# Second phase of a conv-and-FFN kernel: the programs of ACT, GpSimd and SyncE written out for all 32 images

## The chip, the cores and the metric

One core of one Trainium2 chip runs the kernel. The metric is the device time of one execution in microseconds; the kernel before took 2137.33 us, the median of three runs.

## The reference

x is 32 images of 128 channels by 56 x 56. Two residual steps follow each other:

```python
x = x + conv_ref(ln_c(x), w, b, gamma, beta)   # sign(LN over channels) * sign-weights 3x3, batch norm, relu
t = to_tokens(x)                               # 3136 tokens of 128 per image
t = t + ffn_ref(ln_t(t), wr, br, w1, b1, w2, b2)
```

```python
weights = ln_t(t) @ wr + br                    # ffn_ref: router weight per token
sel = the top 1567 tokens of an image by weight
y = gelu(sel @ w1 + b1) @ w2 + b2              # 128 -> 512 -> 128
processed = 0 except y * weight at sel;  result = processed + ln_t(t)
```

The batch norm needs the mean and variance of the convolution over all images, so nothing behind it can begin before all 32 images are convolved.

## The kernel before

Each engine runs a program of its own; semaphores tie them together. Channels lie on the 128 partitions, an image is cut into NCH = 7 chunks of T = 448 tokens. Phase 1 (up to about 500 us) makes the convolution `y` of every image, stores it as f16 in `y_int` and gathers batch statistics. Phase 2 does the rest, image by image, at about 49 us an image.

In phase 2 an order written out by hand rules everything. An image has POS = 56 positions, eight per chunk; in each, TensorE (`PE`) runs `hidden` (L975 to L977: three matmuls of a 128-column block of w1, in two f16 pieces) or `output` (L986). Tables such as RELU_AT, NORM_AT, COUNT_AT say at which position each side job is due: `due(table, shift, n, b, pos)` returns the jobs of image n + shift that fall on `pos`. So while PE multiplies image n, the others prepare images n + 1 and n + 2 and finish n - 1. The side jobs that matter here:

- SyncE (queue `SPq`) in `phase2(n, b)`: writes the statistics rows (three DMAs, L384), writes the router's row to `w_row` (L390), waits until it has landed, loads it back as `wse` for the search (L395) and as `wk` (L397), then loads the second parts of x and y of image n + 2 (L345, L348).
- DVE: `wrow` from the router (L753), then eight rounds of a search for the threshold: `count_above` (L766), summed across partitions by PE (`sum_counts`, L995), `choose`, `raise_end`, `next_candidate` (L772 to L783). Between them it computes token statistics; `mean_over_std` (L714, 112 x 28 elements) reads `stw` and `rm`, and PE's `rows_of_stats` (L951) transposes its result. DVE also forms `base` (L746) and applies the gate (L823).
- GpSimd (`POOL`): `rm` by a power (L444, 4.8 us), `low_part` (L430), `residual` (L425), `add_base` (L437).
- ACT: gelu into `hs` (L517), `yo` out of PSUM (L527), relu into `zr` (L545, which for chunks 0 and 4 waits for the loads of x and y), the f16 copy `th` (L552), and two DMA issues of gate_all (L539).

How each engine runs through the images: `pairs` writes out the images before the third, makes a hardware loop over pairs of images (13 turns, n = 3 to 28) and writes out the last ones. In the loop n is a register, so waits such as `act.wait_ge(h_done, g * NB + j + 1)` need register arithmetic in front of them, and DMA addresses need register moves. Written out, the values are constants in the instructions. DVE's phase 2 is written out for all images already; PE, ACT, GpSimd and SyncE use `pairs`. GpSimd, ACT and SyncE have the same program for image n in either form. Images are named here by the n that PE is working on: PE begins image 1 at about 587 us, image 2 at 637, image 3 at 687, image 16 at 1326, image 28 at 1910, image 29 at 1958.5.

Of the kernel before, what the change touches and what calls it, by code (L numbers as in the profile page):

```python
# [82 lines left out]
def block_kernel(nc, consts, x_in, cw_in, cb_in, gamma_in, beta_in, wr_in, br_in, w1_in, b1_in,  # L83
# [13 lines left out]
    with ExitStack() as ctx:  # L97
# [168 lines left out]
        def wait_count(eng, semaphore, value):  # L266

            if not (isinstance(value, int) and value <= 0):
                eng.wait_ge(semaphore, value)

        def pairs(eng, body, first, last, lo, hi):

            for n in range(lo, first):
                body(n, n % 2)
            turns = (last - first) // 2
            with eng.Fori(0, turns) as k:
                body(k * 2 + first, first % 2)
                body(k * 2 + (first + 1), (first + 1) % 2)
            for n in range(first + 2 * turns, hi):
                body(n, n % 2)  # L280
# [14 lines left out]
        def has(n, low=0, high=n_img):  # L295

            return not is_int(n) or low <= n < high

        def cut(t, c, size=T):
            return t[:, c * size:(c + 1) * size]  # L300
# [3 lines left out]
        def due(table, shift, n, b, pos):  # L304

            steps = [table] if is_int(table) else table
            found = []
            for at, m, mb in ((pos, n + shift, (b + shift) % 2), (pos + POS, n + shift - 1, (b + shift + 1) % 2)):
                if at in steps and has(m):
                    found.append((m, mb, steps.index(at)))  # L310
            return found
# [11 lines left out]
        P2 = (3, n_img - 3)  # L323
# [5 lines left out]
        def _(sp):  # L329
# [73 lines left out]
                    store(n - 1, 1 - b, 0)  # L403
                    store(n - 1, 1 - b, 1)

            pairs(sp, phase2, *P2, -2, n_img + 1)
            for b in range(2):
                sp.wait_ge(out_saved[b], 32 * (n_img // 2))

# [1 line left out]
        @block.gpsimd  # L411
        def _(pool):

            for b in range(2):
                nc.gpsimd.memset(sg[b], 0.0).then_inc(border_clear, 1)
            nc.gpsimd.memset(wsel_h[:, :], 0.0).then_inc(prep_pool, 1)
            nc.gpsimd.memset(wsel_l[:, :], 0.0).then_inc(prep_pool, 1)
            pool.wait_ge(bound_ready, 1)
            nc.gpsimd.tensor_tensor(roots[:, :], norms[:, :], half, ALU.pow).then_inc(bound_rooted, 1)
            pool.wait_ge(var_bn_ready, 1)  # L420
            nc.gpsimd.tensor_tensor(bn_r, bn_ve, kt[:, K_MHALF:K_MHALF + 1], ALU.pow).then_inc(bn_rooted, 1)  # L421

            def residual(n, b, c):
                pool.wait_ge(relu_ready, n * NCH + c + 1)
                nc.gpsimd.tensor_tensor(cut(xb[b], c), cut(xb[b], c), zr[(b + c) % 2][:, :],  # L425
                                        ALU.add).then_inc(x1_ready, 1)

            def low_part(n, b, c):
                pool.wait_ge(th_ready, n * NCH + c + 1)
                nc.gpsimd.tensor_tensor(cut(tl, c), tr[(b + c) % 2][:, :], cut(th, c),  # L430
                                        ALU.subtract).then_inc(tl_ready, 1)

            def add_base(m, b, c):
                g = m * NCH + c
                pool.wait_ge(gated, g + 1)
                pool.wait_ge(base_ready, g + 1)
                nc.gpsimd.tensor_tensor(cut(yo[b], c), cut(yo[b], c), cut(base[b], c),  # L437
                                        ALU.add).then_inc(out_ready, 1)

            def phase2(n, b):  # L440
                for pos in range(POS):
                    for m, mb, _ in due(VAR_AT + 1, 1, n, b, pos):
                        pool.wait_ge(var_ready, m + 1)
                        nc.gpsimd.tensor_tensor(rm[:, 0, :], stw[:, 5, :], kt[0:TILE, K_MHALF:K_END],  # L444
                                                ALU.pow).then_inc(rstd_ready, 1)
                    for m, mb, c in due(RELU_AT, 2, n, b, pos):
                        residual(m, mb, c)
                    for m, mb, c in due(LOW_PART_AT, 1, n, b, pos):
                        if has(m - 1):
                            pool.wait_ge(h_done, ((m - 1) * NCH + c + 1) * NB)  # L450
                            pool.wait_ge(w_done, m)
                        low_part(m, mb, c)
                    for m, mb, c in due([p + 1 for p in OUT_AT], -1, n, b, pos):
                        add_base(m, mb, c)

            pairs(pool, phase2, *P2, -2, n_img + 1)


        @block.scalar
        def _(act):  # L460
# [45 lines left out]
            def phase2(n, b):  # L506
                for pos in range(POS):
                    slot, j = divmod(pos, 2 * NB)

                    if j < NB and has(n):  # L510
                        g = n * NCH + slot
                        act.wait_ge(h_done, g * NB + j + 1)
                        if j == 0:

                            wait_count(act, y_done, g - 1)

                        nc.scalar.activation(hs[(b + slot) % 2][:, j, :], ps[:, H_BANK + j, 0:T],  # L517
                                             ACT.Gelu_apprx_tanh, bias=b1c[:, j:j + 1],
                                             scale=undo[:, 1:2]).then_inc(h_ready, 1)
                    if j == 2 * NB - 1 and (has(n) and slot > 0 or slot == 0 and has(n - 1)):  # L520

                        c = (slot - 1) % NCH
                        m, mb = (n, b) if slot > 0 else (n - 1, 1 - b)
                        act.wait_ge(y_done, m * NCH + c + 1)
                        if c == 0 and has(m - 2):
                            act.wait_ge(out_saved[mb], (m - mb) * 16)
                        nc.scalar.activation(cut(yo[mb], c), ps[:, Y_BANK, 0:T], ACT.Identity,  # L527
                                             bias=b2_c).then_inc(y_taken, 1)
                    for m, mb, _ in due(ROWS_AT, 1, n, b, pos):
                        act.wait_ge(rms_ready, m + 1)  # L530
                        for s in range(PIECES):
                            act.dma_start(rows[32 + s:33 + s, :].rearrange("a (j p) -> a j p", p=TILE),
                                          rms[:, s, 1, :]).then_inc(norm_rows_in, 16)
                    for m, mb, _ in due(GATE_OUT_AT, -1, n, b, pos):
                        act.wait_ge(gate_saved, (m + 1) * 16)
                        if has(m - 1):
                            act.wait_ge(gated, m * NCH)
                        for part in range(2):
                            act.dma_start(gate_all[:, PART[part]], g_dram[bass.ds(m, 1), PART[part]]  # L539
                                          .to_broadcast([C, (HALF, NCH - HALF)[part] * T])).then_inc(gate_in[part], 16)  # L540
                    for m, mb, c in due(RELU_AT, 2, n, b, pos):
                        if c in (0, HALF):
                            act.wait_ge(xy_in[mb][c // HALF], (m - mb) * 16 + 32)
                        wait_count(act, x1_ready, m * NCH + c - 1)
                        nc.scalar.activation(zr[(mb + c) % 2][:, :], cut(y16[mb], c), ACT.Relu,  # L545
                                             bias=bn_t[:, :], scale=bn_s[:, :]).then_inc(relu_ready, 1)
                    for m, mb, c in due(LOW_PART_AT, 1, n, b, pos):
                        if has(m - 1):
                            act.wait_ge(h_done, ((m - 1) * NCH + c + 1) * NB)
                            act.wait_ge(w_done, m)  # L550
                        act.wait_ge(t_ready, m * NCH + c + 1)
                        nc.scalar.activation(cut(th, c), tr[(mb + c) % 2][:, :], ACT.Copy).then_inc(th_ready, 1)  # L552

            pairs(act, phase2, *P2, -2, n_img + 1)

# [504 lines left out]
```

## Time and profile before

| | us |
|---|---|
| three runs, median (lowest, highest) | 2137.33 (2133.52, 2137.93) |
| the profiled execution's own time | 2127.27 |
| its span | 2125.5 |
| PE busy | 1994.1 (94%) |
| DVE / ACT / POOL busy | 1666.4 / 1211.1 / 933.1 |

The profiled execution is 10 us shorter than the median of the runs, 1.8 us of its time lie outside the span. A busy PE in the table is modelled: ends of matmuls overlap the starts of the next, so differences between starts are the safer measure.

### The profile page before, as it was taken

How to read it: one execution, taken by the hardware profiler on the slowest of the kernel's cores; microseconds unless marked ns; L12 is line 12 of the kernel's file. 1: busy time of each engine (PE TensorE's matmuls, PEld its weight loads, DVE VectorE, ACT ScalarE, POOL GpSimd, SP SyncE). 2: the span in 40 equal slices, each digit the busy share in tenths (PEclk: the TensorE clock that was granted, in tenths of full speed). 3: DMA queues.
4: the chain of work that ended last, by engine and by line, in shares of the span. 5: the costliest groups of instructions: out<-in, count | busy, mean ns of one | idle time of the engine just before them, and what ended most of it. 6: DMA issues, size and time to landing. Idle time of an engine off the chain costs nothing. (4 is left out here: it accounts for less than half of the span.)

```text
span 2125.5 us, 35828 instructions
## 1 busy us (share of the span) xinstructions
PE 1994.1 (94%) x9515; PEld 1021.8 (48%) x9515; DVE 1666.4 (78%) x4766; ACT 1211.1 (57%) x2030; POOL 933.1 (44%) x714
## 2 busy tenths in 40 slices
PE   7999999995899999999999999999999999999995
PEld 4555555552444444444444444444444444444442
DVE  6777777775688888877788888888877888888875
ACT  4444444443656566666666666666666656666652
POOL 1000000003455556655556565556655656565543
PEclk9999999997899999999999999999999999999998
DMA  4434344443123332333333333333333333333213
GB/s 163 178 140 181 142 176 154 163 162 111 51 102 122 131 119 111 126 127 112 112 128 117 124 115 124 114 134 111 127 125 112 125 120 129 111 124 124 99 69 124
DMA packets 68726, 267.91 MB, mean 126 GB/s; under 512 B 22352, under 2 KB 27184, under 8 KB 64688
## 3 DMA queue, kind: packets, MB, share of 16 engines
q1 hardware_dynamic: 55264, 214.90, 27.5%
q10 hardware_dynamic: 13392, 52.29, 6.6%
q14 instruction: 52, 0.43, 0.1%
q8 instruction: 18, 0.29, 0.1%
HBM read 188.08 MB, written 77.87 MB: 125 GB/s over the span
## 5 line engine op out<-in xcount | busy, mean ns | idle before, releaser
L986 PE MATMUL ps<-hs,w_c 128*128 128x448 f32 x1792 | 763.7, 553 | 0.6 <-ACT yo L527 0.6
L517 ACT ACTIVATE hs<-ps,b1c,undo 128x448 f32<-128x448 f32 x896 | 609.2, 718 | 127.2 <-PE ps L977 123.4
L986 PEld LDWEIGHTS ps<-hs,w_c 128*128 128x128 f32 x1792 | 313.4, 190 | 208.6 <-issue 176.9
L889 PE MATMUL ps<-yo,cwT 128*128 128x448 bf16 x2016 | 408.7, 355 | 0.0
L430 POOL TENSOR_TENSOR tl<-tr,th 128x448 f16<-128x448 f32 x224 | 244.0, 1090 | 310.5 <-PE ps L977 192.9
L425 POOL TENSOR_TENSOR xb<-xb,zr 128x448 f32<-128x448 f32 x224 | 261.3, 1168 | 269.2 <-ACT zr L545 267.8
L975 PE MATMUL ps<-th,w_h 128*128 128x448 f16 x896 | 319.2, 356 | 19.8 <-ACT hs L517 19.7
L976 PE MATMUL ps<-tl,w_h 128*128 128x448 f16 x896 | 317.1, 354 | 0.0
L977 PE MATMUL ps<-th,w_l 128*128 128x448 f16 x896 | 317.0, 354 | 0.0
L437 POOL TENSOR_TENSOR yo<-yo,base 128x448 f32<-128x448 f32 x224 | 277.7, 1247 | 77.8 <-DVE yo L823 77.8
L527 ACT ACTIVATE yo<-ps,cols 128x448 f32<-128x448 f32 x224 | 141.5, 632 | 241.7 <-PE ps L986 241.4
L889 PEld LDWEIGHTS ps<-yo,cwT 128*128 128x128 bf16 x2016 | 185.9, 97 | 193.5 <-issue 24.3
L494 ACT ACTIVATE y<-ps 128x448 f16<-128x448 f32 x224 | 121.6, 543 | 258.9 <-PE ps L889 258.9
L545 ACT ACTIVATE zr<-y,bn_t,bn_s 128x448 f32<-128x448 f16 x224 | 169.2, 756 | 144.0 <-DMA y<-y_int 128.6
L605 DVE BATCH_NORM_STATS2 base<-y 128x448 f16 (+1 forms) x224 | 140.2, 627 | 118.5 <-ACT y L494 109.0
L729 DVE TENSOR_TENSOR ur<-xb,ps 128x448 f32<-128x448 f32 x224 | 138.5, 618 | 107.5 <-PE ps L966 100.6
L691 DVE BATCH_NORM_STATS2 st<-ps 112x6 f32<-112x128 f32 x896 | 195.1, 282 | 14.3 <-PE ps L931 10.3
L823 DVE TENSOR_TENSOR yo<-yo,gate_all 128x448 f32<-128x448 f32 x224 | 198.0, 887 | 7.9 <-DMA gate_all<-gate_row 7.9
L421 POOL TENSOR_TENSOR sm<-sm,kt 128x1 f32<-128x1 f32 x1 | 0.6, 564 | 452.3 <-DVE sm L679 452.3
L552 ACT ACTIVATE th<-tr 128x448 f16<-128x448 f32 x224 | 129.0, 576 | 106.3 <-DVE tr L738 91.9
L746 DVE SCALAR_TENSOR_TENSOR base<-tr,xb 128x448 f32<-128x448 f32 x224 | 186.7, 834 | 1.2
L444 POOL TENSOR_TENSOR rm<-stw,kt 112x28 f32<-112x28 f32 x32 | 153.5, 4797 | 34.4 <-DVE stw L709 34.4
(132 smaller groups left out, 2324.2 us busy)
## 6 DMA issues: line engine op xcount, KB each, us to landing
xb<-x SPq DMA_DIRECT2D x31, 1568.0 KB, 7.6
xb<-x SPq DMA_DIRECT2D x33, 896.0 KB, 4.5
gate_all<-gate_row ACTq DMA_DIRECT2D x32, 896.0 KB, 4.3
result<-yo SPq DMA_DIRECT2D x32, 896.0 KB, 3.5
y_int<-y SPq DMA_DIRECT2D x32, 784.0 KB, 3.6
xb<-x SPq DMA_DIRECT2D x33, 672.0 KB, 4.3
gate_all<-gate_row ACTq DMA_DIRECT2D x32, 672.0 KB, 5.5
result<-yo SPq DMA_DIRECT2D x32, 672.0 KB, 3.0
```

Of the source, the lines that this page charges most:

```text
L425: nc.gpsimd.tensor_tensor(cut(xb[b], c), cut(xb[b], c), zr[(b + c) % 2][:, :], ALU.add).then_inc(x1_ready, 1)
L430: nc.gpsimd.tensor_tensor(cut(tl, c), tr[(b + c) % 2][:, :], cut(th, c), ALU.subtract).then_inc(tl_ready, 1)
L437: nc.gpsimd.tensor_tensor(cut(yo[b], c), cut(yo[b], c), cut(base[b], c), ALU.add).then_inc(out_ready, 1)
L517: nc.scalar.activation(hs[(b + slot) % 2][:, j, :], ps[:, H_BANK + j, 0:T], ACT.Gelu_apprx_tanh, bias=b1c[:, j:j + 1], scale=undo[:, 1:2]) ...
L691: last = V.bn_stats(st[:, c * TPG + i, :], ps[0:TILE, BC0 + c % 2, i * C:(i + 1) * C])
L746: V.scalar_tensor_tensor(cut(base[b], c), tr[ring][:, :], 1.0 / T_SCALE, cut(xb[b], c), ALU.mult, ALU.add).then_inc(base_ready, 1)
L823: V.tensor_tensor(cut(yo[b], c), cut(yo[b], c), cut(gate_all, c), ALU.mult).then_inc(gated, 1)
L889: last = M(bank, cwT[:, t, :], sg[b][:, c * ROWS + dy:c * ROWS + dy + ROWS, dx:dx + SIDE], start=t == 0, stop=t == TAPS - 1)
L975: M(bank, w1_h[:, blk], cut(th, c), start=True, stop=False)
L976: M(bank, w1_h[:, blk], cut(tl, c), start=False, stop=False)
L977: M(bank, w1_l[:, blk], cut(th, c), start=False, stop=True).then_inc(h_done, 1)
L986: last = M(bank, w2_c[:, j, :], hs[(b + c) % 2][:, j, :], start=first, stop=final)
```

## The change

Three calls of `pairs` in phase 2 become plain Python loops. The engines SyncE, GpSimd and ACT then have no hardware loop there and no register values; all three programs hold the instructions of 35 or so steps one after the other. TensorE's program is as before (13 turns), DVE's too, and phase 1 is not touched.

```diff
@@ SyncE @@
-            pairs(sp, phase2, *P2, -2, n_img + 1)
+            for n in range(-2, n_img + 1):
+                phase2(n, n % 2)
@@ GpSimd @@
-            pairs(pool, phase2, *P2, -2, n_img + 1)
+            for n in range(-2, n_img + 1):
+                phase2(n, n % 2)
@@ ACT @@
-            pairs(act, phase2, *P2, -2, n_img + 1)
+            for n in range(-2, n_img + 1):
+                phase2(n, n % 2)
```

## Rows read from the trace of the kernel before

**Rows 1.** The page: span, and TensorE's busy time with its instructions.

```profile
span 2125.5 us, 35828 instructions
...
PE 1994.1 (94%) x9515; PEld 1021.8 (48%) x9515; DVE 1666.4 (78%) x4766; ACT 1211.1 (57%) x2030; POOL 933.1 (44%) x714
```

**Rows 2.** Waits from 687 to 1958 us: total us, times, longest us.

```profile
PE ps L995 <- DVE junk L766: 35.9, 31, 1.6
...
PE ps L975 <- ACT hs L517: 17.3, 13, 1.9
...
PEld ps L951 <- DVE rm L714: 0.3, 1, 0.3
```

**Rows 3.** The loops' own line, ACT's branch: ns min/median/max, first and last start.

```profile
L276 ACTq COMPARE_BRANCH  x27: 40/45/54, 99.3 to 1960.4; - x27
```

**Rows 4.** Timeline of SyncE's queue, image 2 (written out).

```profile
660.67 2.62 SPq L384 DMA_DIRECT2D rows<-rms  x3
...
665.87 0.69 SPq L395 DMA_DIRECT2D wse<-w_row  x1
...
667.54 0.43 SPq L348 DMA_DIRECT2D y<-y_int  x1
```

**Rows 5.** Timeline of SyncE's queue, image 16 (in the loop).

```profile
1349.28 2.60 SPq L384 DMA_DIRECT2D rows<-rms  x3
...
1354.75 0.73 SPq L395 DMA_DIRECT2D wse<-w_row  x1
...
1356.80 0.35 SPq L348 DMA_DIRECT2D y<-y_int  x1
```

**Rows 6.** Timeline, ACT and PE, image 16: a late landing of y.

```profile
1364.35 0.76 ACT L545 ACTIVATE zr<-y,bn_t,bn_s 128x448 f32<-128x448 f16 x1 [5.79 <-DMA y<-y_int]
...
1365.77 0.36 PE L975 MATMUL ps<-th,w_h 128*128 128x448 f16 x1 [1.93 <-ACT hs L517]
```

**Rows 7.** DVE L714 alone in three windows: from:to, length, busy (times).

```profile
650.00:662.00 12.00, 1.01 (x1) 1.00 0.36 137
...
1975.00:1985.00 10.00, 3.09 (x1) 1.00 0.44 164
687.00:1958.00 1271.00, 26.33 (x26) 1.00 0.33 121
```

**Rows 8.** Timeline of image 1 (all written out but PE's): DVE, POOL, ACT, PE.

```profile
606.97 3.10 DVE L714 SCALAR_TENSOR_TENSOR rm<-stw,rm 112x28 f32<-112x28 f32 x1 [0.33 <-POOL rm L444]
...
606.90 2.03 POOL L430 TENSOR_TENSOR tl<-tr,th 128x448 f16<-128x448 f32 x2
608.88 1.14 POOL L425 TENSOR_TENSOR xb<-xb,zr 128x448 f32<-128x448 f32 x1
...
604.29 0.85 ACTq L539 DMA_DIRECT2D gate_all<-gate_row  x2
...
606.96 0.57 ACT L552 ACTIVATE th<-tr 128x448 f16<-128x448 f32 x1
...
605.68 3.17 PE L986 MATMUL ps<-hs,w_c 128*128 128x448 f32 x8
610.12 0.36 PE L951 MATMUL ps<-kt,rm 112*28 112x112 f32 x2 [1.27 <-DVE rm L714]
```

**Rows 9.** Timeline of image 28 (in the loop): POOL, ACT, PE.

```profile
1929.93 2.13 POOL L430 TENSOR_TENSOR tl<-tr,th 128x448 f16<-128x448 f32 x2
...
1930.38 0.57 ACT L552 ACTIVATE th<-tr 128x448 f16<-128x448 f32 x1
...
1929.03 3.17 PE L986 MATMUL ps<-hs,w_c 128*128 128x448 f32 x8
1932.04 0.36 PE L951 MATMUL ps<-kt,rm 112*28 112x112 f32 x2
```

**Rows 10.** Timeline of image 2 (written out): ACT.

```profile
654.39 1.01 ACTq L539 DMA_DIRECT2D gate_all<-gate_row  x2
...
657.23 0.57 ACT L552 ACTIVATE th<-tr 128x448 f16<-128x448 f32 x1
```

## The prediction

> **What bounds the kernel now.** I read the page first: PE is busy 94% of the span [rows 1], so the change, which takes nothing from PE, can only move what PE waits for. The waits of the stretch in which ACT, GpSimd and SyncE run in their loops (687 to 1958 us, 26 images) name two: the search's counts on DVE, 35.9 us, and gelu's output on ACT, 17.3 us in 13 waits [rows 2]. That is 53 of 1271 us. Then I followed each wait back in the timelines.
>
> The second leads to a DMA. In image 16 ACT stood 5.79 us at relu L545 for y, and PE's L975 waited 1.93 us for the gelu queued behind it [rows 6]. y is loaded by L348, the last DMA of a chain that SyncE issues without a pause, from the rows L384 on: L384, w_row, its landing, wse, wk, x, y. The first count (L766) waits for wse from the same chain. SyncE's issue time is therefore on the path of both waits, and there the registers cost something.
>
> The before trace also holds a sample of the kernel after: images 1, 2 and 29 are written out on all three engines, as all images will be (image 0 has no image in front of it, and 30 and 31 load none behind them, so I leave these out). Every term below is read as written-out image against loop image.
>
> **SyncE.** From the first L384 to the issue of wse: 665.87 - 660.67 = 5.20 us written out, 1354.75 - 1349.28 = 5.47 in the loop; to the issue of y, 6.87 against 7.52 [rows 4, 5]. So wse leaves 0.27 us earlier, y 0.65 us earlier.
> - y: only late landings make PE wait, 13 in the stretch [rows 2], on average 17.3 / 13 = 1.3 us, more than 0.65. If the landing moves with the issue, 13 x 0.65 = 8.5 us are gained. Below: nothing, if what holds the transfer up is tied to other work and not to its issue. Above: the same with all 17.3 us. I take 8.5.
> - wse: at most 26 x 0.27 = 7.0 us. But behind the first count stands DVE's own work up to the second, and PE meets that next. Nearest to it are the written-out images themselves, where the trace's waits at L995 are about as large as in the loop (35.9 / 26 = 1.4 us an image there). I take 1.5 us, bounds 0 and 7.0.
>
> **ACT and GpSimd.** Their register instructions run in front of the instruction that needs them and mostly beside work of their own engine; neither is the bound (57% and 44% busy, [rows 1]), and PE waits for ACT only as above. For waits at small margins I add 1 us. Sum of gains: 8.5 + 1.5 + 1 = 11 us; bounds 1 and 25 (17.3 + 7.0 + 1).
>
> **What the change takes away besides: the gaps.** L714 is a small DVE instruction, 112 x 28 elements. In the loop it takes 26.33 / 26 = 1.01 us, every time [rows 7]. In image 1 it takes 3.10 us [rows 8], in image 29 3.09, in image 2 1.01 [rows 7]. In image 1 GpSimd's two L430 follow each other without a gap (2.03 us for two) and L425 is next at 608.88, ending at 610.02; L714 begins with the first of them and ends at 610.07. It got its turn only after the third. In image 28 the same three GpSimd instructions are there, but the two L430 take 2.13 us: the second waited for th, which ACT finished at 1930.38 + 0.57 = 1930.95, as the first L430 ended [rows 9]; in this gap L714 gets in. In image 1 th was ready at 607.53, 0.4 us before the first L430 was over [rows 8]. What delays ACT in the loop is the register work ahead of the gate DMAs L539 and of L552. Written out, it is gone, and the gap with it.
>
> The Trainium skill (GPSIMD Engine Reference, Key points) says that GpSimd shares its SBUF interfaces with VectorE and contends with DVE instructions that have two SBUF inputs. L714 has two (stw and rm), and the trace agrees, with 3.10 against 1.01 us; that DVE can lose two turns in a row the page does not say.
>
> The price: PE's L951 transposes L714's result. From the start of the block of eight L986 to L951 pass 610.12 - 605.68 = 4.44 us in image 1 [rows 8] and 1932.04 - 1929.03 = 3.01 in image 28 [rows 9]. So 1.43 us for PE at each lost turn. Nothing behind it gives this back, since PE then runs its fixed order on.
>
> How often? Two of three written-out images lost, images 1 and 29, one after the start-up, one behind 26 loop images, and within 10 ns alike. So I take this as the pattern of a written-out image, not as chance. Image 2 won, though its ACT program is the same: its two L539 issues took 1.01 us instead of 0.85, and L552 came 0.17 us after L714's start instead of with it [rows 8, 10]. I call this an occasional hiccup of ACT's queue and expect it in few images; estimate: 24 of 26 images lose. 24 x 1.43 = 34.3 us. Bounds: 0 and 26 x 1.43 = 37.2.
>
> **Sum.** 2127.27 (the profiled execution's own time) + 34.3 - 11 = 2150.6, so + 23 us. The three runs lie 10 us above that execution; late landings of y vary from run to run, and more of them would give the SyncE term a little more to save. I take 3 us off: 2137.33 + 23.3 - 3 = 2157.6, say 2158.
>
> **Rivals.**
> - *Half the images lose the turn.* Speaks for it: image 2. ACT's order relative to L714 decides at a margin of some tenths of a us. 13 x 1.43 - 11 = + 7.6, so 2145.
> - *The lost turns stay rare* (other side): SyncE's earlier loads decide. Image 2 would be the rule, and 1 and 29 the exceptions at the edges. It speaks against it that 1 and 29 have different neighbours and the same picture. With none lost: 2137.3 - 11 = 2126. The point of decision is 11 / 1.43 = 8 images of 26: below that the change is faster.
> - *Nothing moves*: landings of y are bound to other traffic, and one of the waits on DVE or the second count takes over at once, turns lost rare: 2137, within 0.2% (4.3 us, about what a measurement of this kernel can tell from no change).
> - *The loops' branches cost a fetch of code.* The trace's branch takes 45 ns, at most 54 [rows 3], and no wait of PE stands at it. The Trainium skill (Runtime: NRT & Kernel Launch, Instruction fetch mechanics) says that a taken branch whose target isn't in the two resident pages forces a DMA fetch, and that kernels therefore prefer full unrolling. If each of 13 turns cost one more exposed wait of the longest that rows 2 shows for L995, 1.6 us, the gain would be 11 + 21 = 32 us, 2105 without lost turns. By that rule the change looks clearly good; here the loops' bodies show no such stall.
>
> **How the numbers follow.** Most images lose: 0.60 (own range 2148 to 2168). Half lose: 0.15, of which nearly all slower by over 0.2%. Rare: 0.16, faster. Nothing moves: 0.06. Fetch: 0.03, faster. So faster 0.19, same 0.07, slower 0.74. The range for 8 in 10 takes in the first two, with 2168 widened by 4 us for waits at the fourth count that a written-out image may add, and the unchanged case: 2130 to 2172. It leaves out the faster cases.
>
> **What would show it.** L714 at about 3.1 us in most of the 26 images (sum of 32 near 87 us instead of 36), and PE waiting for it at L951 some 1.3 us each, 24 to 28 times. SyncE's 6.87 us from L384 to L348 in all images. PE's waits at L975 for ACT smaller by 0.65 us each. Register instructions and branches gone from ACTq, POOLq and SPq. Wrong would be: L714 at 1.01 in the middle of the phase, because ACT's lead over GpSimd there differs from images 1 and 29; or a new loss, for instance L746 or L823 held up by GpSimd in the same way, which would make it slower still.

## The result, and the profile after

| | before | after |
|---|---|---|
| median (lowest, highest; 14 runs each, same chips) | 2132.88 us (2128.59, 2137.93) | 2148.81 us (2139.82, 2153.93) |
| ratio, 95% interval | | 1.0069 [1.0053, 1.0085] |
| profiled execution, its span | 2127.27, 2125.5 | 2141.67, 2139.8 |

The change makes the kernel slower by 0.69%: 15.9 us between the medians, 14.3 us between the two profiled spans. The kernel before came out 4.5 us lower in these runs than in the three that the prediction started from.

Each of the three loops that went was one line, now two. From GpSimd's program on, the line numbers are shifted: GpSimd's by 1 (L430 is L431), ACT's by 2 (L552 is L554), DVE's and PE's by 3 (L714 is L717, L951 is L954).

The page of after. TensorE has the same work; instructions fell from 35828 to 33392 (the loops' register work and branches); DVE is busy 46.6 us longer than before [rows 1] with the same number of instructions:

```profile
span 2139.8 us, 33392 instructions
...
PE 1993.9 (93%) x9515; PEld 1018.8 (48%) x9515; DVE 1713.0 (80%) x4766; ACT 1213.9 (57%) x2030; POOL 946.1 (44%) x714
```

TensorE's waits of after in the same 26 images (687 to 1975 us; line waited at, line waited for, total us, times, longest):

```profile
PE ps L998 <- DVE junk L769: 30.8, 48, 1.7
PE ps L954 <- DVE rm L717: 29.5, 23, 1.6
PE ps L978 <- ACT hs L519: 5.9, 5, 1.8
```

Against [rows 2] nearly the whole result is in these three lines. The two waits behind SyncE's chain fell, the counts from 35.9 to 30.8 us and gelu's output from 17.3 to 5.9: 16.5 us gained. A wait that was not there (0.3 us) is now 29.5 us in 23 images. Their sum is + 12.7, of the 14.3 us of span.

`mean_over_std` in all of after (times of one: min, median, max in ns), and who waited for it:

```profile
L717 DVE SCALAR_TENSOR_TENSOR rm<-stw,rm x32: 583/3088/3096, 522.9 to 2043.0; 112x28 f32<-112x28 f32 x32
...
  PE ps L954: 42.4, 27
```

In the same 26 images alone (window, length, its busy time and times):

```profile
687.00:1975.00 1288.00, 74.10 (x26) 1.00 0.33 119
```

27 of the 32 instructions make TensorE wait: the 23 lost ones of the middle, those of images 0, 1 and 29, and the first one of the phase, which takes 1.11 us but is waited for for 8.5 us.

In [rows 7] it was 26.33 us for 26. (74.10 - 26.33) / 2.08 us = 23 images lost their turn. That DVE's busy time grew by nearly the same amount, 46.6 us, is an accident. Over all 32 instructions L717 grew by 50.1 us (36.0 to 86.1). `base` is held less (L749 168.0 us, L746 186.7 before) and so is the gate (192.2, 198.0 before). And one more small DVE instruction with two SBUF inputs, the first of the token statistics, is held: 30.7 us in all instead of 12.3 (min, median and max 208, 350 and 1057 ns before).

```profile
L707 DVE TENSOR_TENSOR stw<-st x32: 209/1049/1155, 516.5 to 2036.6; 112x28 f32<-112x28 f32 x32
```

This second hold is not what costs the time: no wait of TensorE stands behind it, it is there in e2 (median 1051 ns), which is as fast as before, and in e11 (1052), which is faster.

Timeline of image 16 of after, which loses:

```profile
1346.12 3.17 PE L989 MATMUL ps<-hs,w_c 128*128 128x448 f32 x8
1347.34 2.02 POOL L431 TENSOR_TENSOR tl<-tr,th 128x448 f16<-128x448 f32 x2
1347.35 0.57 ACT L554 ACTIVATE th<-tr 128x448 f16<-128x448 f32 x1
1347.41 3.09 DVE L717 SCALAR_TENSOR_TENSOR rm<-stw,rm 112x28 f32<-112x28 f32 x1 [0.33 <-POOL rm L445]
...
1349.32 1.13 POOL L426 TENSOR_TENSOR xb<-xb,zr 128x448 f32<-128x448 f32 x1
1350.55 0.36 PE L954 MATMUL ps<-kt,rm 112*28 112x112 f32 x2 [1.27 <-DVE rm L717]
```

And of image 18, one of three in the middle that win:

```profile
1445.50 3.17 PE L989 MATMUL ps<-hs,w_c 128*128 128x448 f32 x8
1446.72 2.07 POOL L431 TENSOR_TENSOR tl<-tr,th 128x448 f16<-128x448 f32 x2
1446.79 1.01 DVE L717 SCALAR_TENSOR_TENSOR rm<-stw,rm 112x28 f32<-112x28 f32 x1 [0.32 <-POOL rm L445]
1447.02 0.57 ACT L554 ACTIVATE th<-tr 128x448 f16<-128x448 f32 x1
1448.51 0.36 PE L954 MATMUL ps<-kt,rm 112*28 112x112 f32 x2
```

What to see: everything but the start of `th` is alike. It starts 0.06 us before L717 in image 16 and 0.23 us after it in image 18. In image 16 the two L431 take 2.02 us and L717 ends behind the third GpSimd instruction; in image 18 they take 2.07, and L717 gets in at once. From the block of eight L989 to L954 pass 1350.55 - 1346.12 = 4.43 us against 1448.51 - 1445.50 = 3.01: 1.42 us for PE. This difference, the start of `th` less the start of `mean_over_std`, is called the margin below.

SyncE's queue in image 2 of after, to be laid beside [rows 4]: the chain L384 to L348 is 6.80 us there (6.87 before):

```profile
659.72 2.60 SPq L384 DMA_DIRECT2D rows<-rms  x3
...
664.87 0.65 SPq L395 DMA_DIRECT2D wse<-w_row  x1
...
666.52 0.43 SPq L348 DMA_DIRECT2D y<-y_int  x1
```

### The profile page after: what moved, and what is told of

It reads as the page before. It is cut to its first block, busy times and chain, and to the rows that moved or that the text cites. A ratio compares the mean times of both kernels' runs of the same rounds, so it can differ in the third digit from the quotient of the medians.

```text
span 2139.8 us, 33392 instructions
## 1 busy us (share of the span) xinstructions
PE 1993.9 (93%) x9515; PEld 1018.8 (48%) x9515; DVE 1713.0 (80%) x4766; ACT 1213.9 (57%) x2030; POOL 946.1 (44%) x714
## 4 chain that ended last, share of the span: by engine, by line
PE 36%; DVE 15%; DMA 8%; POOL 6%; SPq 5%; issue 5%; ACT 0%; DVEq 0%; POOLq 0%; ACTq 0%
PE ps L989 16%; POOL rm L445 6%; PE ps L934 4%; DMA wse<-w_row 4%; PE ps L978 4%; PE ps L980 4%; PE ps L979 4%; DVE rm L717 4%; SPq L384 4%; DMA w_row<-wrow 3%; DVE base L749 2%; PE ps L967 2%; DVE stw L707 1%; DMA y<-y_int 1%; DVE st L694 1%
## 5 line engine op out<-in xcount | busy, mean ns | idle before, releaser
L989 PE MATMUL ps<-hs,w_c 128*128 128x448 f32 x1792 | 764.9, 553 | 0.6 <-ACT yo L529 0.6
L989 PEld LDWEIGHTS ps<-hs,w_c 128*128 128x128 f32 x1792 | 313.5, 190 | 207.1 <-issue 173.2
L431 POOL TENSOR_TENSOR tl<-tr,th 128x448 f16<-128x448 f32 x224 | 255.2, 1145 | 311.7 <-ACT th L554 297.6
L826 DVE TENSOR_TENSOR yo<-yo,gate_all 128x448 f32<-128x448 f32 x224 | 192.2, 861 | 7.8 <-DMA gate_all<-gate_row 7.8
L554 ACT ACTIVATE th<-tr 128x448 f16<-128x448 f32 x224 | 129.0, 576 | 113.4 <-DVE tr L741 85.1
L749 DVE SCALAR_TENSOR_TENSOR base<-tr,xb 128x448 f32<-128x448 f32 x224 | 168.0, 750 | 1.2
```

Source lines behind the costliest of these rows:

```text
L749: V.scalar_tensor_tensor(cut(base[b], c), tr[ring][:, :], 1.0 / T_SCALE, cut(xb[b], c), ALU.mult, ALU.add).then_inc(base_ready, 1)
L989: last = M(bank, w2_c[:, j, :], hs[(b + c) % 2][:, j, :], start=first, stop=final)
```

## The experiments

All ratios are to the kernel before, run on the same chip between the runs of the experiment. "Lost" is the number of images 3 to 28 in which `mean_over_std` takes about 3.1 us instead of 1.01. Its line is L714 to L720 according to the lines that an edit adds.

| kernel | median us | ratio, 95% | lost of 26 |
|---|---|---|---|
| after | 2148.81 | 1.0069 [1.0053, 1.0085] | 23 |
| e1 ACT alone | 2160.89 | 1.0127 [1.0107, 1.0147] | 23 |
| e2 GpSimd alone | 2132.46 | 1.0011 [1.0000, 1.0021] | 0 |
| e3 SyncE alone | 2114.96 | 0.9922 [0.9909, 0.9936] | 0 |
| e4 all, and a wait on GpSimd | 2121.09 | 0.9953 [0.9937, 0.9970] | 0 |
| e5 all, one input | 2146.39 | 1.0074 [1.0053, 1.0095] | 23 |
| e6 ACT and GpSimd | 2142.06 | 1.0056 [1.0037, 1.0076] | 11 |
| e7 SyncE, and the wait | 2110.16 | 0.9907 [0.9881, 0.9932] | 0 |
| e8 e7, wk issued last | 2106.52 | 0.9893 [0.9866, 0.9920] | 0 |
| e9 all, ACT one step later | 2146.77 | 1.0094 [1.0074, 1.0114] | 23 |
| e10 all, one input, accumulating | 2105.45 | 0.9903 [0.9881, 0.9925] | 0 |
| e11 all, ACT three steps later | 2112.13 | 0.9918 [0.9894, 0.9941] | 0 |
| e12 all, two inputs, accumulating | 2151.52 | 1.0098 [1.0074, 1.0122] | 24 |

### Which of the three loops: e1, e2, e3

One engine's loop is written out, the other two stay as before.

```diff
@@ ACT (e1), GpSimd (e2) or SyncE (e3), one of the three @@
-            pairs(act, phase2, *P2, -2, n_img + 1)
+            for n in range(-2, n_img + 1):
+                phase2(n, n % 2)
```

> Only ACT is written out; GpSimd and SyncE keep their loops. Theory A (the lost turn of L714 comes from ACT's th being ready before GpSimd's first L430 ends): the two L430 follow each other without a gap, L714 takes about 3.1 us in most of the 26 images (sum over 32 above 70 us), PE waits for it some 20 times, and the time is 25 to 35 us above the kernel before, more than with all three, since SyncE's earlier loads are not there. Rival B (GpSimd's own register work makes the gap): L714 stays at 1.01 us and the time within 4 us of before. Rival C (straight-line code costs fetches): a third or so of the 16 us, about 5 to 8 us slower, with L714 at 1.01 us.

> Only GpSimd is written out. Theory A: ACT still delays th, the second L430 still waits for it, L714 stays at 1.01 us, time within 4 us of before. Rival B: L714 at 3.1 us in most images and 25 to 35 us slower. Rival C: about 3 to 6 us slower with L714 at 1.01 us.

> Only SyncE is written out. Theory A: from the first L384 to the issue of y 6.87 us instead of 7.5, wse 0.27 us earlier, PE's waits for ACT at L975 smaller by about 8 us, L714 at 1.01 us; 8 to 15 us faster than before. Rival C: slower by 2 to 5 us. Rival D (the loads are hidden or tied to other traffic): within 4 us.

ACT's loop alone brings the whole loss: 1.27%, with `mean_over_std` held in 23 images and TensorE's wait for it at 42.6 us in all (11.1 before), while the two other waits are as in the kernel before (42.5 and 19.7 over the whole span):

```profile
PE ps L996 <- DVE junk L767: 42.8, 39, 1.8
PE ps L952 <- DVE rm L715: 42.6, 27, 8.5
PE ps L976 <- ACT hs L517: 20.6, 19, 2.0
```

GpSimd alone does nothing: the interval touches 1, nothing is lost, and `th` starts 1346.55 - 1346.33 = 0.22 us behind `mean_over_std`. SyncE alone is the whole gain, 0.78%:

```profile
PE ps L996 <- DVE junk L767: 35.3, 52, 1.9
...
PE ps L976 <- ACT hs L518: 12.5, 11, 1.9
```

Counts 42.5 to 35.3 and gelu's output 19.7 to 12.5: 14.4 us of the 16.3 between the medians. The issue of y, counted from `wrow` and averaged over 26 images, went from 6.16 to 5.38 us in e3 (5.37 in after), that of wse from 4.11 to 3.74 (3.73 in after). The three parts add up to + 1.27 + 0.11 - 0.78 = + 0.60%, against 0.69% for the whole, inside its interval. But that is luck, since the parts are not independent: ACT and GpSimd together (e6, below) give + 0.56, not + 1.38, and SyncE's part on top of them adds 0.13 where it takes 0.78 away alone.

### Is it the lost turn, and does it wait for a gap: e4, e7, e9, e11

e4 keeps the change and makes GpSimd let DVE go first, before the second of the two `low_part`:

```diff
@@ GpSimd, due(LOW_PART_AT, ...) @@
+                        if c == NCH - 1 and has(m + 1):
+                            pool.wait_ge(mr_ready, m + 2)
```

> All three written out, and GpSimd's L430 of the last chunk waits for L714 (mr_ready) before it starts, so that DVE has its turn between the two L430. Theory A: L714 at about 1.0 us in every image, no PE wait at rows_of_stats, 30 to 35 us faster than with all three written out, so 12 to 20 us faster than the kernel before. Rival C: L714 at 1.0 us, but the time stays near that with all three written out, 10 to 16 us above before. Rival E (DVE's lost 2 us an image are made up elsewhere): a gain below 15 us against the changed kernel.

Nothing is lost any more, and the time falls from 1.0069 to 0.9953, 25 us: the lost turn is the cause of the slowdown. But it is less than the 33 us of 23 turns. Image 16 of e4:

```profile
1341.27 1.04 POOL L431 TENSOR_TENSOR tl<-tr,th 128x448 f16<-128x448 f32 x1
...
1341.33 1.01 DVE L719 SCALAR_TENSOR_TENSOR rm<-stw,rm 112x28 f32<-112x28 f32 x1 [0.33 <-POOL rm L445]
1342.58 1.03 POOL L431 TENSOR_TENSOR tl<-tr,th 128x448 f16<-128x448 f32 x1 [0.27 <-DVE rm L719]
...
1343.57 1.13 POOL L426 TENSOR_TENSOR xb<-xb,zr 128x448 f32<-128x448 f32 x1
...
1344.27 0.55 DVE L727 CAST rms<-rrest 28x224 bf16<-28x224 f32 x1
```

The wait moves GpSimd's own second `low_part` and `residual` back, `residual` now to 1344.70, and there it meets the next small DVE instruction, the cast in `split_stats`, which takes 0.55 us instead of 0.26 or 0.27. SyncE's chain begins behind it: counted from `wrow`, wse leaves at 4.03 and y at 5.67 us (means over 26 images; 3.73 and 5.37 in after). TensorE pays at both waits:

```profile
PE ps L1000 <- DVE junk L771: 44.3, 60, 1.6
PE ps L980 <- ACT hs L521: 19.6, 17, 1.3
```

The other way to open the gap is ACT's side. e9 puts one small activation, which waits for nothing, in front of `th` of the last chunk; e11 puts three.

```diff
@@ e9; e11 has the activation three times, each with a buffer of its own @@
+        pad = [sb(f"pad{b}", [C, 1], f32) for b in range(2)]
...
@@ ACT, due(LOW_PART_AT, ...) @@
                         act.wait_ge(t_ready, m * NCH + c + 1)
+                        if c == NCH - 1:
+                            nc.scalar.activation(pad[mb][:, :], kt[:, 0:1], ACT.Copy)
                         nc.scalar.activation(cut(th, c), tr[(mb + c) % 2][:, :], ACT.Copy).then_inc(th_ready, 1)
```

> All three written out, and one tiny instruction more on ACT in each image (a copy of 128 x 1), in front of the L552 of the last chunk, about 0.2 us. Nothing waits for it but ACT's own L552. Theory A (what decides is the start of this L552 against the start of L714: lost at -0.01 us and before, won at +0.13 us and after in the runs so far): L552 moves from -0.06 to about +0.15 us, L714 takes 1.01 us in nearly all images, PE's wait at rows_of_stats goes, and the kernel becomes 20 to 30 us faster by an added instruction. Rival: the loss comes from something else that goes with a written-out ACT: L714 stays at 3.09 us and the time at 16 us above before.

e9 missed: 1.0094, and nothing won. The expectation had taken for granted that one activation is enough. Image 15 of e9 shows that it was not:

```profile
1304.77 2.02 POOL L432 TENSOR_TENSOR tl<-tr,th 128x448 f16<-128x448 f32 x2
1304.77 0.20 ACT L556 ACTIVATE pad<-kt 128x1 f32<-128x1 f32 x1
1304.84 3.09 DVE L720 SCALAR_TENSOR_TENSOR rm<-stw,rm 112x28 f32<-112x28 f32 x1 [0.32 <-POOL rm L446]
1304.87 0.57 ACT L557 ACTIVATE th<-tr 128x448 f16<-128x448 f32 x1
```

The margin went from - 0.06 to + 0.03 us only, since ACT begins the next instruction before the 0.20 us are over, and the two L432 still take 2.02 us. In the three images of e9's middle that win, the margin is 0.22, 0.33 and 0.49. Either the dose was too small, or ACT's timing merely goes along with the loss. e11 tells the two apart:

> All three programs written out, and three small ACT activations (about 0.2 us each, none waits) in front of the last chunk's th; one of them moved th to 0.03 us after the start of L714, where 23 images still lost. Gap theory (L714 gets in whenever GpSimd has to wait for th before its second low_part): three move th to about +0.3 to +0.4, beyond the +0.13 at which images won in the run with SyncE looped, so L714 is at 1.01 us in 24 or more of the 26 images, TensorE's waits for it fall to one, and the time is 20 to 30 us below the kernel after, 2118 to 2130. If ACT's timing only went along with the loss and something else in the written-out programs causes it: L714 at 3.09 in 20 or more, and 2146 to 2150.

```profile
1336.87 2.06 POOL L432 TENSOR_TENSOR tl<-tr,th 128x448 f16<-128x448 f32 x2
1336.88 0.38 ACT L556 ACTIVATE pad<-kt 128x1 f32<-128x1 f32 x3
1336.93 1.01 DVE L720 SCALAR_TENSOR_TENSOR rm<-stw,rm 112x28 f32<-112x28 f32 x1 [0.33 <-POOL rm L446]
1337.15 0.57 ACT L557 ACTIVATE th<-tr 128x448 f16<-128x448 f32 x1
```

The margin is + 0.22 us, all 26 images win, and the time is 2112.13, 0.9918: 1.51%, 32 us, below after, more than the expected 20 to 30. This is the 33 us of 23 turns; no wait was taken away, and work was added. So, with all three programs written out, `th` being early is what costs the kernel its time. Neither of DVE's later instructions is disturbed, and SyncE's chain leaves as early as in after (3.75 and 5.39 us); TensorE's waits for counts and gelu are 38.0 and 10.9 us over the whole span, 15 less than in e4.

e7 is e3 with GpSimd's wait of e4 (SyncE written out, ACT and GpSimd in their loops).

> Only SyncE written out (16.3 us faster), and the wait of GpSimd's last L430 for L714. The wait can act only in the images that are written out on ACT, 0, 1 and 29, which lost their turn: 3 x 1.43 = 4.3 us more, so 19 to 22 us faster than before. If the wait itself costs GpSimd and so th and tl something in every image: nothing more, or some us back.

It gives 0.9907, against 0.9922 without the wait, with intervals that overlap. In e3 only images 0, 1 and 29, outside of ACT's and GpSimd's loops, had still lost.

### Do SyncE and GpSimd matter for the loss: e6

ACT and GpSimd are written out, SyncE keeps its loop.

> ACT and GpSimd written out, SyncE keeps its loop. If the parts add up: 29.7 (ACT) + 1.2 (GpSimd) = 31 us slower than before, L714 at 3.1 us in 22 to 25 of the 26 images. Rival: if ACT and GpSimd in step make a worse or a better pattern, 36 us and more, or 25 and less.

The expected + 31 us did not come, but the better pattern of its rival: it is 1.0056, 11 us above before, and 11 images are lost instead of 23, all of them with an even number. Images 15 and 16 of e6, three lines each:

```profile
1299.08 2.03 POOL L430 TENSOR_TENSOR tl<-tr,th 128x448 f16<-128x448 f32 x2
1299.14 1.01 DVE L716 SCALAR_TENSOR_TENSOR rm<-stw,rm 112x28 f32<-112x28 f32 x1 [0.32 <-POOL rm L444]
1299.28 0.57 ACT L553 ACTIVATE th<-tr 128x448 f16<-128x448 f32 x1
...
1348.81 2.02 POOL L430 TENSOR_TENSOR tl<-tr,th 128x448 f16<-128x448 f32 x2
1348.86 0.57 ACT L553 ACTIVATE th<-tr 128x448 f16<-128x448 f32 x1
1348.87 3.09 DVE L716 SCALAR_TENSOR_TENSOR rm<-stw,rm 112x28 f32<-112x28 f32 x1 [0.32 <-POOL rm L444]
```

Even images have a margin of - 0.01 and lose (18 and 26 have + 0.27 and + 0.13 and win), odd ones + 0.13 to + 0.15, one + 0.23, and win. ACT's gate DMAs wait for SyncE's store of the mask, and in SyncE's loop that store comes 0.16 us later in the first image of a turn, the odd one (read from the starts in the trace; not tried by itself). So the part of the edit that brings the gain, SyncE's, also takes away a delay that protected half of the images.

It protects them only where GpSimd is written out too. e1 differs from e6 in GpSimd's loop alone. Its margins are the same, + 0.14 in the odd images and - 0.01 in the even ones, and yet it loses the odd ones as well. Image 15 of e1:

```profile
1310.13 2.03 POOL L430 TENSOR_TENSOR tl<-tr,th 128x448 f16<-128x448 f32 x2
1310.20 3.10 DVE L715 SCALAR_TENSOR_TENSOR rm<-stw,rm 112x28 f32<-112x28 f32 x1 [0.32 <-POOL rm L444]
1310.34 0.57 ACT L552 ACTIVATE th<-tr 128x448 f16<-128x448 f32 x1
```

So the margin alone does not decide. In images 1 to 29, with GpSimd written out, images lost up to + 0.06 us (e9's image 1) and won from + 0.11 (e5's image 9). With GpSimd in its loop, they lost up to + 0.15 (12 odd images of e1) and won from + 0.18 (e1's image 26). Image 0 does not fit either: it lost at + 0.11 in e1, e3 and e12 and won at + 0.11 in e2. One difference shows in GpSimd's queue: in e6 a semaphore instruction of 43 ns (L429) stands between the end of `th` and the second L430, in e1 none does. Whether that is the reason was not tried. Against e1, writing out GpSimd as well takes the time from 1.0127 to 1.0056, though alone it does nothing.

### What form of instruction is held: e5, e10, e12

The rule that the prediction weighed names two SBUF inputs. Three forms of the same small instruction, all with the three programs written out:

```diff
-                V.scalar_tensor_tensor(rm[:, 1, :], mean2, 0.5, rm[:, 0, :], ALU.mult, ALU.mult)
@@ e5: one input; the factor rm is left out of the result @@
+                V.tensor_scalar(rm[:, 1, :], mean2, 0.5, None, ALU.mult)
@@ e10: one input and a sum beside it; the factor rm is left out of the result @@
+                V.tensor_scalar(rm[:, 1, :], mean2, 0.5, None, ALU.mult, ALU.add, accum_out=acc[:, :])
@@ e12: both inputs and a sum beside it; the whole computation @@
+                V.scalar_tensor_tensor(rm[:, 1, :], mean2, 0.5, rm[:, 0, :], ALU.mult, ALU.mult, accum_out=acc[:, :])
```

> All three written out, and L714 reads one SBUF tensor instead of two: a tensor_scalar of mean2 by 0.5, without the factor from rm (so the mean over std is left out of the result), same wait, same output tile. Theory A with the Trainium skill's rule (GPSIMD Engine Reference, Key points: contention is with DVE instructions that have two SBUF inputs): it runs beside GpSimd's L430, about 0.2 us from first to last, no PE wait at rows_of_stats, and the time falls by 25 to 35 us against the changed kernel, to 8 to 15 us below the kernel before. Rival F (any DVE instruction waits behind GpSimd in a row): it stays at 3.1 us and the time at 16 us above.

> As the kernel with L714 reading one SBUF tensor (factor from rm left out), but in the accumulating form that L766 uses, a form that took 621 us/1000 each time in all traces, beside any GpSimd work. If DVE must take its turn with GpSimd only in some forms (two SBUF inputs, and the plain one-input form that still took 3.08 us), this one runs beside L430: about 0.2 us, no PE wait at rows_of_stats, and the time 20 to 35 us below the kernel with all three written out. If every DVE instruction that comes at this point is held: 3.1 us again, 15 us above before.

> All three programs written out, the whole computation kept, L714 with both of its SBUF inputs, and an accumulator output that nobody reads (one more column of sums). If it is the accumulating form that gets past GpSimd, as in the run with one input: L714 about 0.2 to 0.3 us without the loss, TensorE's waits for it one, 2104 to 2118, the time of the kernel after less 30 to 43. If two SBUF inputs are held in this form as well (one input was what freed it there): L714 at 3.09 us or so in 20 or more images and 2140 to 2150. Between them, held but for one turn: about 1 us each image, 2115 to 2125.

The instruction in each (e5, e10, e12), with min, median and max in ns:

```profile
L717 DVE TENSOR_SCALAR rm<-stw x32: 565/3078/3083, 523.3 to 2047.8; 112x28 f32<-112x28 f32 x32
```

```profile
L718 DVE TENSOR_SCALAR_CACHE_REDUCE rm<-stw x32: 168/182/183, 524.9 to 2006.4; 112x28 f32<-112x28 f32 x32
L718 DVE DVE_READ_ACCUMULATOR rm<-stw x32: 76/82/84, 525.0 to 2006.5; 112x1 f32 x32
```

```profile
L718 DVE SCALAR_TENSOR_TENSOR rm<-stw,rm x32: 576/3090/3095, 524.8 to 2053.5; 112x28 f32<-112x28 f32 x32
```

The plain form with one input is held as long as that with two. With one input and an accumulator it is not held at all, 0.18 us in each of 32 images, and the time falls to 0.9903. With two inputs the accumulator does not help. So neither the number of inputs nor the accumulator decides alone: held are two inputs, with the accumulator or without, and one input in the plain form. The Trainium skill (SBUF — State Buffer, Who interferes with whom) says just this: a DVE instruction with two SBUF inputs contends with a GpSimd instruction that reads SBUF, and `tensor_scalar` can contend too, since it can enter a mode that takes the shared pair of ports, but "not the form that also writes out its accumulator". The three runs agree, with 3.09, 3.08 and 0.18 us. The expectation of e5 had left the case of the plain form out, and missed. What mode the plain form ran in no row shows.

e10 also shows how short such an instruction is when nothing holds it. The 1.01 us of a winning image look to be mostly waiting too, for one GpSimd instruction (1.01 to 1.04 us) instead of three.

### The best version: e8

e7, and on SyncE the load of `wk`, which nobody needs soon, is issued after x and y instead of before them.

```diff
@@ SyncE @@
-                    sp.dma_start(wk[:, :], w_n.rearrange("a (r t) -> (a r) t", t=MR_COLS)).then_inc(w_mask_in, 16)
@@ behind the loads of x and y @@
+                if has(n):
+                    sp.dma_start(wk[:, :], w_n.rearrange("a (r t) -> (a r) t", t=MR_COLS)).then_inc(w_mask_in, 16)
```

> As the one with SyncE written out and the wait, and SyncE issues the load of wk after x and y instead of before them, so that x and y leave 0.5 us earlier and wse as before. If the landing of y moves with its issue and late landings are what PE waits for: PE's waits for ACT at L975 fall by another 0.5 us each, 3 to 6 us faster. If late landings are tied to other traffic: no change within 2 us.

y leaves 4.93 us after `wrow` instead of 5.41. Of TensorE's longest waits that for gelu's output is gone (8.9 us in e7); behind the counts come only single long ones of phase 1 and of the first images:

```profile
PE ps L999 <- DVE junk L770: 42.0, 63, 2.1
PE ps L883 <- DVE xl L589: 14.7, 3, 13.1
PE ps L935 <- POOL xb L427: 9.2, 4, 8.0
PE ps L955 <- DVE rm L718: 8.5, 1, 8.5
```

The time is 2106.52, 0.9893 of before, with the whole computation: 1.1% faster than before and 1.8% faster than after. Against e7 the intervals overlap, so of this last step only the direction is likely.

## Why the prediction was right, and where it was off

The direction and its cause were right, and the time is in the range; by size it was 9 us too high (2158 for 2148.81). 4.5 us of this is the kernel before, lower in the new runs; 4.8 us is the change itself, + 15.9 instead of + 20.7.

- **The lost turn, count.** 24 of 26 were predicted, 23 happened; images 9, 18 and 26 won. Reading images 1 and 29 of the trace before as the pattern of all written-out images, and image 2 as a hiccup, held. Shown as the cause of the slowdown by e4 and e11.
- **The lost turn, price.** 1.43 us each; measured 1.42. 23 x 1.42 = 32.7 us instead of 34.3. Nothing later gave it back. It was not the only DVE instruction that was held (L707, + 18.4 us in all), but the only one that TensorE waited for.
- **The gap as the mechanism.** The prediction put it on ACT's register work in front of L539 and L552. e1 and e2 confirm the engine: ACT's loop alone brings the loss, GpSimd's nothing. e6, laid beside after and e1, adds what the prediction had missed: SyncE's register work, through the mask's store, is part of the same delay, and whether a given delay is enough depends on GpSimd's own form. The prediction took the longer time of the two L430 (2.13 us in image 28) for the gap that lets L714 in; but L714 also got in where they took 2.03 us, in image 2 of before and in e6's odd images, the same as in images that lost. What the runs show is that ACT's `th` must come late enough; the gap itself is seen in some winning images only. e9 missed on its dose and e11 settled that ACT's delay is enough.
- **The SyncE term was sized too small.** This is the step that was off. The sum had 8.5 + 1.5 us. TensorE's waits fell by 11.4 us for gelu (17.3 to 5.9) and by 5.1 for counts (35.9 to 30.8), 16.5 us together, and e3 alone gives 16.3 between medians. For y the assumption was that each of 13 late landings is 0.65 us shorter; in fact y leaves 0.79 us earlier (6.16 to 5.37), and what fell is the number of waits, 13 to 5, not the size of one (17.3 / 13 = 1.3 us, 5.9 / 5 = 1.2). Why a landing is mostly either in time or late by as much as before was not tried. For wse the prediction argued that the next count would take the gain back, from written-out images whose waits at L995 looked as large as the loop's; 5.1 of at most 7.0 us came through.
- **ACT's and GpSimd's own register work, + 1 us.** e2 at 1.0011 and e1's two other waits, unchanged, say that it is about nothing in direct time; GpSimd's form does matter for the turns once ACT is written out (e1 against e6).
- **The 3 us taken off** for the runs above the profiled execution went the right way, but cannot be told apart in these runs.
- **Half lost.** Not in after, but it is what e6 does, with SyncE in its loop and GpSimd written out: 2142.06, close to the 2145 of that rival. The closeness is luck, as e6 also lacks the gain of SyncE's part, which the 2145 has in it.
- **Rare, or nothing moves.** Excluded by the 23.
- **A fetch of code at the loops' branches.** It predicted that writing out pays some 21 us. e2 gives + 0.11% and e1 a loss fully accounted for by the turns; only SyncE gains, and there the waits that shrink are those behind its issue. The instruction queue of the page moved 73 packets instead of 52, 0.60 MB instead of 0.43, without a wait of TensorE that would belong to it. The Trainium skill (Runtime: NRT & Kernel Launch, Instruction fetch mechanics) says that kernels prefer full unrolling, for the fetch at a taken branch; the runs show no stall here that it could have removed.
- **The feared waits at later counts or at L746 and L823** did not come: the wait for counts fell, and both instructions took less time than before (168.0 us for 186.7, 192.2 for 198.0).

## What to carry to other kernels

When a change makes an engine early, ask which gap in another engine its lateness had opened. Here an ACT instruction that came 0.4 to 0.6 us earlier (margin + 0.38 and + 0.55 before, - 0.06 after) let GpSimd's instructions follow one another, a DVE instruction of 0.2 us then took 3 us with its wait for a turn, and the slower edit hid a faster one (SyncE alone, 0.9922). A trace whose first and last images are already in the new form is a sample of the change: compare them with the others instruction by instruction. And split an edit over several engines into one run for each before judging it, then run the pairs too: here the single runs added up by luck, and the pair did not.

## What the runs showed of the hardware that was not expected

- A small DVE instruction that is ready 0.07 us after a GpSimd instruction began can wait not only for that one but for the two that follow it without a gap: 3.09 us behind three, 1.01 behind the first alone (after, images 16 and 18). Whether it gets in cannot be read from GpSimd's rows: the two L430 take 2.02 or 2.03 us in images that lose and in images that win (e6, images 15 and 16; e1, image 15; e5, image 9).
- What shows beforehand is how long before the end of GpSimd's first instruction the input of its second is ready. With GpSimd written out, `th` ready 0.34 us ahead or more lost (e9, image 1, the closest), 0.29 us ahead or less won (e5, image 9). With GpSimd in its loop 0.25 us ahead still lost (e1, image 13), and 0.22 us ahead won (e1, image 26). These are read from the single instructions of images 1 to 29.
- One activation of 0.20 us in front of another on ACT delayed it by some 0.09 us (margin - 0.06 to + 0.03), three delayed it by 0.28.
